# Gated feed-forward weights: sums made by adding DMAs in DRAM, rounded halves kept in DRAM for the second token pair

## What is computed

```python
h = silu(x @ w_gate) * (x @ w_up)          # w_gate, w_up: 512 x 2048
h_sparse = _sparsify_2to4(h)               # of each 4 neighbours the 2 largest in magnitude are kept
x = _layernorm(x + h_sparse @ w_down)      # w_down: 2048 x 512
```

## Time and profile before

| | us |
|---|---|
| runs | 1162.85, 1158.88, 1153.5; median 1158.88 |
| profiled execution | 1152.48 |
| its span, first to last instruction | 1150.7 |
| TensorE busy with matmuls | 1023.0 (89%) |
| VectorE busy | 888.2 (77%) |
| ScalarE busy | 605.0 (53%) |
| GpSimd busy | 536.5 (47%) |

### The profile page before, as it was taken

How to read it: one execution, slowest core, us unless ns; L and a number is a source line. 1 busy time by engine, 2 the same in 40 slices (tenths; PEclk the granted TensorE clock), 3 DMA queues, 4 the chain that set the end, 5 groups by cost and what they waited for, 6 DMA issues and landing times.

```text
span 1150.7 us, 18114 instructions
## 1 busy us (share of the span) xinstructions
PE 1023.0 (89%) x5830; PEld 817.5 (71%) x5831; DVE 888.2 (77%) x1889; ACT 605.0 (53%) x1141; POOL 536.5 (47%) x640
## 2 busy tenths in 40 slices
PE   7989999998999769999986998889959989899886
PEld 6667777776777648788775876767747767678665
DVE  5898799688778865665759486675988889777894
ACT  5787588578758952234364323453543423544424
POOL 2194457347445613223457355563443557445224
PEclk9999999999999989999998998999979989899998
DMA  8877277356716632233321332221201212103001
GB/s 265 247 203 183 85 194 219 102 180 175 193 59 175 212 109 65 75 121 135 101 74 37 38 73 37 8 67 37 74 3 34 74 37 91 51 14 101 18 20 73
DMA packets 61081, 116.78 MB, mean 101 GB/s; under 512 B 6976, under 2 KB 9024, under 8 KB 60992
## 3 DMA queue, kind: packets, MB, share of 16 engines
q1 hardware_dynamic: 56112, 101.48, 32.2%
q0 software_dynamic: 4880, 14.18, 3.2%
HBM read 84.69 MB, written 30.94 MB: 100 GB/s over the span
## 4 chain that ended last, share of the span: by engine, by line
PE 34%; DVE 13%; ACT 5%; DMA 5%; issue 4%; POOL 2%; SPq 1%; POOLq 0%; DVEq 0%; ACTq 0%
PE f_bank L53 20%; PE f_bank L1955 12%; DVE h_lo L2356 4%; DMA w_raw<-gate 3%; ACT h_hi L2120 2%; DMA wd_raw<-down 2%; DVE beats L2323 2%; ACT w_hi L2047 1%; DVE h L2347 1%; PE f_bank L1829 1%; ACT wd_hi L2055 1%; DVE h L2299 1%; ACT h L2102 1%; PE f_bank L1837 1%; DVE x_lo_T L2267 1%
## 5 line engine op out<-in xcount | busy, mean ns | idle before, releaser
L53 PE MATMUL f_bank<-wd_hi,h_hi 128*128 128x512 f32 x256 | 109.0, 426 | 48.8 <-DVE h_lo L2356 43.4
L714 ACT ACTIVATE probs<-bank,nmax 128x384 f32<-128x384 f32 (+3 forms) x256 | 131.7, 549 | 21.4 <-DVE nmax L899 19.2
L883 DVE CUSTOM_DVE_ANT_0 bank<-bank,mask 128x384 f32<-128x384 f32 (+3 forms) x256 | 123.0, 502 | 13.7 <-PE bank L510 12.8
L521 PE MATMUL bank<-ident,probs 128*128 128x128 f32 x640 | 108.7, 284 | 24.5 <-DVE pt_lo L908 11.1
L908 DVE TENSOR_TENSOR pt_lo<-bank,pt_hi 128x512 f16<-128x512 f32 (+1 forms) x192 | 114.8, 598 | 16.7 <-ACT pt_hi L724 16.3
L2097 ACT ACTIVATE h<-f_bank 128x512 f32<-128x512 f32 x64 | 37.4, 596 | 165.1 <-PE f_bank L1955 163.7
L724 ACT ACTIVATE pt_hi<-bank 128x512 f16<-128x512 f32 (+1 forms) x192 | 104.9, 546 | 23.4 <-PE bank L521 22.9
L1740 POOL TENSOR_TENSOR w_lo<-w_raw,w_hi 128x512 fp32r<-128x512 f32 x48 | 82.7, 1738 | 63.4 <-ACT w_hi L2047 63.3
L1955 PE MATMUL f_bank<-x_hi_T,w_hi 128*128 128x512 f32 x256 | 101.4, 396 | 6.7 <-ACT h L2097 2.7
L53 PE MATMUL f_bank<-wd_lo,h_hi 128*128 128x512 f32 x256 | 106.5, 416 | 0.0
L53 PE MATMUL bank<-x_hi,w_qk 128*128 128x512 f32 x256 | 100.7, 412 | 6.2 <-DVE x_lo L913 5.7
(11 more groups left out here) (275 smaller groups left out, 2928.1 us busy)
## 6 DMA issues: line engine op xcount, KB each, us to landing
big_lo<-q_hi_dram SPq DMA_DIRECT2D x32, 256.0 KB
big_lo<-q_lo_dram SPq DMA_DIRECT2D x32, 256.0 KB
big_lo<-k_hi_dram SPq DMA_DIRECT2D x32, 256.0 KB, 3.7
big_lo<-k_lo_dram SPq DMA_DIRECT2D x32, 256.0 KB, 5.2
w_raw<-up SPq DMA_DIRECT2D x32, 256.0 KB, 3.6
w_raw<-gate SPq DMA_DIRECT2D x32, 256.0 KB, 4.5
wd_raw<-down SPq DMA_DIRECT2D x32, 256.0 KB, 3.9
rows<-sorted_dram SPq DMA_DIRECT2D x19, 256.0 KB, 2.6
```

The lines of the kernel that those rows point to most:

```text
L53: ins = pe.matmul(out, a(k, i), b(k, j), start=(n == 0), stop=(n == len(chain) - 1))
L521: ins = pe.transpose(TP[u % TR][:, j * P:(j + 1) * P], probs[u % RP][:, j * P:(j + 1) * P], ident[:, :])
L714: ins = act.activation(probs[u % RP][:, at:at + cols(r)], S[u % SR][:, at:at + cols(r)], ACT.Exp, bias=nmax[:, r, c:c + 1])
L883: dve.tensor_tensor_reduce(out=S[u % SR][:, at:at + cols(r)], in0=S[u % SR][:, at:at + cols(r)], in1=mask[:, T - cols(r):T], scale=1.0, sc ...
```

## The change

- **Layout and sums.** The host hands gate and up over in another order, two rows of blocks by eight rounds. The four sums of all eight rounds are made once in DRAM (`sums_dram`): SP issues four copies of 2 MB, DRAM to DRAM, right behind the first three loads of expert rows, and GpSimd adds the second operands by sixteen accumulating DMAs of 512 KB during the expert tiles (`sum_weights`: two behind tile 0, one each behind tiles 2 and 4, three each behind tiles 6, 7, 9 and 12). GpSimd's first waits, behind `place(0)`, until all four copies have landed; those behind tiles 2 and 4 wait for earlier adds, those behind tile 9 for the three of tile 6, those behind tile 12 for the three of tile 9.
- **Loads and stores by group.** Each of the seven groups is loaded by itself (`weight_in`, 256 KB) as soon as its product b of the round before is done. In rounds 0 to 7 both halves of each group are also stored to `kept_dram` (`weight_out`, 2 x 256 KB), and in rounds 8 to 15 the halves are loaded from there ready made; there are no `weight_hi` and `weight_lo` for them.
- **Engines.** `weight_lo` is VectorE's alone, 7 instructions in a round. GpSimd keeps `down_lo`, the layer norms and the scatters. Gate of block 0 isn't added any more: `copy` puts product 1 into bank FB, products 2a and 2b add to it there, and `silu` reads it with a scale of -1 (the token blocks B11, B21, B22 are negated). `add_product` of 11 goes, on either column group.
- **Order.** In an even round VectorE's whole chain of d = L - 1 stands first and `kept_lo(L - 2)` next, ahead of `add_product(L, "22a")`; in odd rounds `kept_lo` stands there too and the chain stays in `behind`. `kept_hi` moves ahead of `copy(L, "7a")` on ScalarE. There are three `mag` buffers in turn.

```diff
+            def weight_in(L, X):
+                n = weight(L, X)
+                if X in "5673":
+
+                    sp.wait_ge(s_order, SUMMED[L > 1])
+                if n >= RW:
+
+                    sp.wait_ge(s_wraw[n % RW], wraw_count(n - RW))
                 if L > 0:
 
-                    sp.wait_ge(*wlo_ready(L - 1, GROUPS - 1))
-                    sp.wait_ge(*wlo_ready(L - 1, GROUPS - 2))
+                    sp.wait_ge(s_pr, product_done(L - 1, X + "b"))
+                if 0 < L <= 2 * NCH:
+
+                    sp.wait_ge(s_wst[(n - NW) % 2], 32 * ((n - NW) // 2 + 1))
+                if L >= 2 * NCH:
+                    for i in range(2):
+                        sp.dma_start(both(aw[i], X).bitcast(F32),
+                                     kept_dram[i, L - 2 * NCH, FREED.index(X)].rearrange("p (i n) -> p i n", i=2)).then_inc(s_wraw[n % RW], 16)
+                    return
+                sp.dma_start(both(raw, X), weight_source(L, X)).then_inc(s_wraw[n % RW], 16)
...
+            def weight_out(L, X):
...
+                sp.wait_ge(*wlo_ready(L, X))
                 for i in range(2):
+                    sp.dma_start(kept_dram[i, L, FREED.index(X)].rearrange("p (i n) -> p i n", i=2),
+                                 both(aw[i], X).bitcast(F32)).then_inc(s_wst[n % 2], 16)
...
             for n in range(3):
                 load(n, n)
-            weights_in(0)
+            for n, of in enumerate((up[0], up[0], gate[0], gate[1])):
+                sp.dma_start(sums_dram[n].rearrange("u p n -> (u p) n"),
+                             of.rearrange("u p n -> (u p) n")).then_inc(s_draw, 16)
...
+            for L in range(1, ROUNDS):
+                for X in FREED:
+                    store_until(weight(L, X) - 3)
+                    weight_in(L, X)
...
+            def sum_weights(at, of, units, waits):
+
+                wait_apart(pool, s_passed, waits)
+                for u in units:
+                    pool.dma_start(sums_dram[at, u:u + 2].rearrange("u p n -> (u p) n"),
+                                   of[u:u + 2].rearrange("u p n -> (u p) n"), accum_op=ALU.add,
+                                   max_dma_last_dim=8192).then_inc(s_order, 16)
+
+            FIRST, OTHERS = (0,), (2, 4, 6)
+            sums_at = {0: ((0, up[1], FIRST, [(s_draw, COPIED)]), (1, gate[0], FIRST, [(s_draw, COPIED)])),
+                       2: ((2, sums_dram[0], FIRST, [(s_order, 32)]),),
+                       4: ((3, sums_dram[2], FIRST, [(s_order, 48)]),),
+                       6: ((0, up[1], OTHERS, [(s_order, SUMMED[0])]),),
+                       7: ((1, gate[0], OTHERS, [(s_order, SUMMED[0])]),),
+                       9: ((2, sums_dram[0], OTHERS, [(s_order, SUMMED[0] + 96)]),),
+                       12: ((3, sums_dram[2], OTHERS, [(s_order, SUMMED[0] + 144)]),)}
...
             for n in range(NS):
                 ln2.rstd(pool, n, n % 4, False)
                 place(n)
-                if n == 2:
-                    weight_sums(0)
-                if n in first_group and first_group[n] % 2 == 1:
-                    weight_lo(0, first_group[n])
-
+                for sum_of in sums_at.get(n, ()):
+                    sum_weights(*sum_of)
...
-            def weight_lo(L, g):
-                i, j = group_blocks[g]
-                dve.wait_ge(s_whi, GROUPS * L + g + 1)
...
+            def weight_lo(L, X):
+                dve.wait_ge(s_whi, weight(L, X) + 1)
```

More of the change, by code:

```diff
@@ L1486, in late @@
             free_slots = [hslot[2 * (d // 2) + half, d % 2] for half in range(2)] + free_slots
-    assert all(hslot[L, r] < 6 for L in range(ROUNDS - 1) for r in range(2))
     with ExitStack() as ctx:
@@ L1607, in late @@
         NTURN = 2 * RW
-        first_group = {12 + g: g for g in range(GROUPS)}
+        first_weight = {12 + i: X for i, X in enumerate(FREED)}
+        MADE = 2 * NCH
+        COPIED = 16 * 4
+        SUMMED = (16 * 4, 16 * 16)
         def chunk(L):
@@ L2135, in round_ @@
                 s, odd = divmod(L, 2)
-                more = L + 1 < ROUNDS
-                soon = L >= 3 and odd and more
+                more = L + 1 < MADE
                 copy(L, "1a")
-                copy(L, "1b")
-                if L == 0:
-                    token_hi(0, "T4")
-                    token_hi(0, "B22")
                 if L == LB + 1:
@@ L2168, in round_ @@
                     magnitudes(s - 1, 1, 1)
-                for g in range(2 if soon else 0, 4) if more else ():
-                    weight_hi(L + 1, g)
-                silu(L, 0, 1)
-                for g in (4, 5) if more else ():
-                    weight_hi(L + 1, g)
                 if L == LB:
@@ L2181, in round_ @@
                 silu(L, 1, 1)
-                if more:
-                    weight_hi(L + 1, 6)
+                for X in ("7", "2", "4") if more else ():
+                    weight_hi(L + 1, X)
                 if L == LB:
@@ L2190, in round_ @@
                     magnitudes(s, 0, 1)
+                if more:
+                    weight_hi(L + 1, "3")
             for n in range(2):
```

353 lines of the change are left out of this document (176 added, 177 removed).

## The result

The changed kernel takes 1182.38 us (median of 4 runs), the one before 1156.19 on the same chip: the ratio is 1.0223, with a 95% interval of 1.0184 to 1.0263. It is slower by 2.2%, where 1128 us were forecast (2.4% less than 1156.19), and it lies outside the range given (1100 to 1170). The profiled execution has a span of 1178.9 us against 1150.7.

A forecast was written before the change was run, and what follows sets the result against it. TensorE was taken to idle ahead of down products for a late `kept_lo`, then run at half clock. Terms 29 + 8 - 19 - 15 - 23 - 7 = -27 took 1152.5 to 1125.5 us, forecast as 1128, range 1100 to 1170.

The forecast's parts named there:

- The expert stage: Expert tiles: copies stall GpSimd and tile 1's norm, 21 us; half clock 2, adds 6; +29 us, bounds +11 and +65.
- Start of the rounds: Rounds 0 and 1: `copy` of 1a delays 2a and group 3's loads aren't covered; net +8 us, bounds 0 and +15.
- 2a "near 560.2": Round 0: 2a, waiting for `copy` of 1a, comes at 560.2 at the earliest instead of about 555.2; +5 us.
- Rounds 2 to 6: Even rounds take 32 us and odd ones 30, so four periods take 124 us against 143.0; -19 us.
- the third rival: First pair's rounds: weight loads wait behind stores and come late, +40 us, about 1168 us in all; chance 0.10.
- The boundary: 774.4 to 858.0: the 6.85 us wait, its half clock and half of 5.02 us go; -15 us, bounds -5 and -20.
- Rounds 8 to 13: With weight halves loaded ready made, five periods take 152.5 us against 175.6; -23 us.
- The end: From the down product at 1033.6 on: 105.2 us become 98; -7 us, bounds -2 and -10.
- its own 0.6%: Whole kernel: the profiled execution, 1152.5 us, lies 0.6% under the median of the runs, 1158.9.
- Copies and adds: Rival on the expert tiles: copies and adds hidden, costing 11 us instead of 29, about 1109 us in all; chance 0.20.
- slow adds: Rival on the expert tiles: adding DMAs run at 60 GB/s, GpSimd waits 44 us instead of 6, about 1166; chance 0.15.
- the change of name of the wait: Rival in the rounds: 3a waits for the 22 sums as down products did for `kept_lo`, about 1156 us; chance 0.12.

The follow-up runs named there:

- splitting the chain: Changed kernel with late scatters, where in even rounds only `compare` of the chain stays ahead of the 22 sums on VectorE: ratio 0.9739 to the kernel before.

## Why the prediction was wrong, point by point

**The expert stage (+29).** +29.9, and that it comes out so near is luck: 23 us were forecast for the copies and 6 for the adds, and leaving them out gives 16 and 13.6. The copies stall tile 3 by 13.01 us and not 21. The wait ended with the load of that tile's rows, which stands behind the copies, and not with `norm(1)`, whose path through GpSimd the sum went by. GpSimd waited 10.45 us for the copies, which had landed some 29 us after their issue.

```profile
424.60 1.24 SPq L1737 DMA_DIRECT2D sums_dram<-up  x2
```

```profile
454.09 0.95 POOL L1777 DMA_DIRECT2D sums_dram<-up  x1 [10.45 <-DMA sums_dram<-gate]
...
519.86 2.58 POOL L1777 DMA_DIRECT2D sums_dram<-sums_dram  x3 [0.25 <-issue]
```

8.4 MB in 29 us are 290 GB/s: nearer to the bound of one pass, 24.5 us, than to the middle that was taken, 37. The Trainium skill's figure ("DMA: Bandwidth & Descriptors", section "Latency and other measured facts"), 207 to 214 GB/s, is for copies of tiles of 128 rows of 16 KiB. An estimate from it made it 40 us; the trace shows 29 for these copies, which are laid out otherwise, and it decides. The stall of GpSimd behind tile 9, which I put at 6, is 0.25. The adds cost by another way: they slow the loads of tile rows and of the token blocks (waits at 510.74, 532.89, 537.97 and 562.13, of 1.5 to 4.4 us). In the run without adds these four waits are gone.

**Start of the rounds (+8).** +13.8. The mechanism was right: 7.77, 5.13 and 5.25 us for `copy` of 1a, 18.1 in all, and the old waits of 2.05, 3.73 and 4.31 are gone, which is 8.1 net. The 22 sums of round 2 add little, since they were waited for before as well, for 5.79 us and now for 7.38:

```profile
618.38 0.80 PE L1955 MATMUL f_bank<-x_hi_B,w_hi 128*128 128x512 f32 x1 [5.79 <-DVE h L2299]
```

What the sum had put at nothing is the clock behind these waits. The same 269 matmuls take 69.9 us instead of 65.0, at a mean granted clock of 0.84 instead of 0.94 (579.74 to 675.15, and 549.80 to 631.40 before). One reading in the sum doesn't fit itself: 2a "near 560.2" lies ahead of the 560.7 to which ScalarE is busy; round 0 lost 5.7 us where 5 were put.

**Rounds 2 to 6 (-19).** +20.4, and two steps failed. The first is the one that read "16 to 19 us at 343 GB/s of 30, so it should fit", under the third rival. The rate came from the earlier trace rows, a stretch without scatters. The earlier trace rows had the other rate beside it, and I read past it: 631.4 to 774.4 shows a share of 0.31 for 45 GB/s, against 0.13 for 38 in the next row, 145 and 292 GB/s at a full share. The same transfers cost twice there. In the list of DMA issues for that stretch alone, loads take 9 to 11 us to land, and not the 3.6 of the earlier trace rows, a median over the whole program. Before the change TensorE waited for none of these loads; GpSimd did, 47.0 us in four waits, while it was busy for 79 of the 143. That the scatters are what makes the stretch slow shows in the kernel before without them, where the same 45 GB/s come at a share of 0.14 and the loads land in 3.0 to 3.7 us (columns as in the earlier trace rows):

```profile
631.04:772.63 141.59, 127.67 (x528) 103.76 (x528) 107.32 (x133) 57.43 (x92) 56.84 (x38) 0.93 0.14 45
```

The change puts stores beside them, a load behind each store's wait, and `weight_lo` ahead of `add_up` on VectorE. Leaving out scatters gives back 26.1 us of these rounds, moving them 27.0. The third rival (weight traffic late, 0.10) is the case that came, though in two bursts and not as 5 us in six rounds.

The second step is "with GpSimd nearly idle it takes at most 9.8 us": the chain doesn't run beside an idle GpSimd but beside `down_lo`, which the even rounds keep. 1.3 us of wait became 6 to 7, and splitting the chain gave back 12.1 us. Chain and `kept_lo` were 3.2 us longer than the sum had them in round 4; the rest of the 5.2 us is not traced to a term. Together 27.0 and 12.1 are the 39 us of the difference, and rounds 2 to 6 then take 124.3. That this meets the forecast 124 is in part chance, since the version that does so has another order on VectorE than the one that was forecast.

**The boundary (-15).** -12.7. The 5.02 us at 846.26 went whole. I took the 6.85 us ahead of the down product of round 8 as gone, but 5.93 us remain at 909.43. Two things end just ahead of it:

```profile
902.40 6.93 POOL L1794 TENSOR_TENSOR wd_lo<-wd_raw,wd_hi 128x512 fp32r<-128x512 f32 x4 [69.22 <-ACT wd_hi L2089]
...
904.02 4.18 DVE L2394 TENSOR_TENSOR h_lo<-h,h_hi 128x1024 fp32r<-128x1024 f32 x2
```

`kept_lo`, which in that round still stands behind `gated_first`, ends at 908.20, and `down_lo` at 909.33, 0.1 us ahead of the down product. `down_lo` came last, and no term of the sum had it as a wait.

**Rounds 8 to 13 (-23).** -17.3: here the order pays as argued, the ready-made halves never make TensorE wait, and of 158.3 us 154.2 are matmuls. Rounds 9 and 11 take 32.6 and 33.9 us where 30 was forecast (down products at 909.43, 942.03, 972.94 and 1006.84), the second with a wait of 2.01 for the 22 sums; the other three are as forecast. `kept_lo` still takes 1442 ns on average where 1180 was foreseen.

```profile
L2394 DVE TENSOR_TENSOR h_lo<-h,h_hi 128x1024 fp32r<-128x1024 f32 x10 | 14.0, 1442 | 25.0 <-ACT h_hi L2157 25.0
L2385 DVE SCALAR_TENSOR_TENSOR h<-wins,h 128x512 f32<-128x512 bf16 x20 | 12.5, 688 | 0.1
```

**The end (-7).** -6.0.

**The sum.** By its own 0.6% the 1125.5 us make 1132 and not 1128. Against an error of 55 us this is nothing.

**The rivals.** Copies and adds are not hidden; slow adds did not come (0.25 us behind tile 9 where that rival had 33); the change of name of the wait (0.12) came in part, as 22 sums. The sign was lost by giving the traffic of the first pair 0.10 on the strength of a median.

## What to carry to other kernels

Before transfers are added to a stage, read for that stage what a full DMA share moves, and its own landing times; a rate from another stage and a median over the program hide exactly the stretches in which DMA is slow. Look for small scatters there: they cost little by themselves and much to whoever runs beside them, so put them where transfers are issued a whole round ahead of need. And when an engine is relieved of work, ask which of its small instructions now come earlier, beside which operations of the others its last large work falls, and who waits for that work once the old wait is gone.
